# Quantised feed-forward weights rebuilt in the attention stage and kept in HBM, instead of beside their matmuls; a new order of TensorE's work in local attention

## The reference

```python
x = x + tanh(g_xattn[0]) * local_attention(ln(x), ctx)      # 8 heads, window of 16 positions along the 512 axis
x = x + tanh(g_ffn[0])   * routed_lora(ln(x))               # x @ W_base + top-2 of 8 experts of rank 16
x = x + tanh(g_xattn[1]) * rotary_attention(ln(x), ctx)     # 32 query heads, 8 key heads of 128, batches of 64
x = x + tanh(g_ffn[1])   * gated_mlp(ln(x))                 # silu(x @ Wg) * (x @ Wu) @ Wd, 512 -> 1376 -> 512
# the three matrices of the last block are 4-bit numbers, eight packed in an int32 along k:
W[k, n] = scales[g_idx[k], n] * (w4[k, n] - (z4[g_idx[k], n] + 1))
```

## Time and profile before

| | us |
|---|---|
| median of 3 runs | 1184.46 (1182.89 to 1184.77) |
| the profiled execution's own time | 1184.0 |
| its span, first to last instruction | 1182.2 |
| busy: PE, DVE, POOL, ACT | 1065.9, 799.2, 425.9, 363.2 |
| local attention, routed lora | 0 to 268, 268 to 344 |
| rotary attention, gated mlp, down | 344 to 944, 944 to 1118, 1118 to 1182 |

### The profile page before, as it was taken

How to read it: one execution, slowest core, us unless ns; L and a number is a source line. 1 busy time by engine, 2 the same in 40 slices (tenths; PEclk the granted TensorE clock), 3 DMA queues, 4 the chain that set the end, 5 groups by cost and what they waited for, 6 DMA issues and landing times. The chain is left out here.

```text
span 1182.2 us, 13680 instructions
## 1 busy us (share of the span) xinstructions
PE 1065.9 (90%) x4894; PEld 754.7 (64%) x4894; DVE 799.2 (68%) x1230; ACT 363.2 (31%) x938; POOL 425.9 (36%) x262
## 2 busy tenths in 40 slices
PE   5677778778578999999999999999999789999998
PEld 1333333335456777777777777777777457777787
DVE  4888888858876766667677666766665456666423
ACT  3333333213212443334333333432333222111121
POOL 4566666646423433424334233333330012111121
PEclk8888889978788999999999999999999979999999
DMA  8000000000320110101111010110200012111001
GB/s 264 1 1 2 1 1 3 10 0 19 103 57 27 45 45 28 39 26 45 45 29 52 11 63 28 45 45 18 64 1 1 1 43 56 54 54 52 14 1 72
DMA packets 46143, 43.21 MB, mean 37 GB/s; under 512 B 7646, under 2 KB 35046, under 8 KB 46076
## 3 DMA queue, kind: packets, MB, share of 16 engines
q1 hardware_dynamic: 45356, 41.97, 11.7%
q10 hardware_dynamic: 720, 0.36, 0.1%
HBM read 40.22 MB, written 2.10 MB: 36 GB/s over the span
## 5 line engine op out<-in xcount | busy, mean ns | idle before, releaser
L1240 POOL TENSOR_TENSOR shared<-shared 128x512 f32<-128x512 f32 x64 | 82.3, 1286 | 201.6 <-DVE shared L1367 201.4
L1365 DVE TENSOR_TENSOR shared<-ps,cs 128x512 f32<-128x512 f32 x80 | 55.2, 690 | 95.7 <-PE ps L765 95.7
L1302 ACT ACTIVATE c_xn<-c_xn,c_mn 128x64 f32<-128x64 f32 x256 | 86.1, 337 | 106.0 <-DVE c_mn L1381 106.0
L763 PE MATMUL ps<-woh,oh 128*128 128x512 f32 x256 | 103.7, 405 | 5.1 <-DVE ol L1397 5.1
L763 PE MATMUL ps<-xh,wqh 128*128 128x512 f32 x256 | 106.6, 417 | 0.4 <-DVE shared L1367 0.4
L1402 DVE SCALAR_TENSOR_TENSOR x<-ps,gate,x 128x512 f32<-128x512 f32 x64 | 48.0, 751 | 79.4 <-PE ps L765 79.4
L765 PE MATMUL ps<-woh,ol 128*128 128x512 f32 x256 | 101.4, 396 | 0.0
L764 PE MATMUL ps<-wol,oh 128*128 128x512 f32 x256 | 101.2, 395 | 0.0
L765 PE MATMUL ps<-xh,wql 128*128 128x512 f32 x256 | 100.6, 393 | 0.0
L764 PE MATMUL ps<-xl,wqh 128*128 128x512 f32 x256 | 99.9, 390 | 0.0
L549 DVE TENSOR_TENSOR r<-ps,vpad 128x512 f32<-128x512 f32 x128 | 79.4, 683 | 28.8 <-PE ps L638 28.8
(11 more groups left out here) (181 smaller groups left out, 2475.2 us busy)
## 6 DMA issues: line engine op xcount, KB each, us to landing
stage<-in_wq SPq DMA_DIRECT2D x16, 512.0 KB, 3.7
stage<-in_wo SPq DMA_DIRECT2D x16, 512.0 KB, 3.6
qraw<-in_gate_qweight SPq DMA_DIRECT2D x40, 64.0 KB, 2.3
qraw<-in_up_qweight SPq DMA_DIRECT2D x40, 64.0 KB, 2.3
qraw<-in_down_qweight SPq DMA_DIRECT2D x10, 256.0 KB, 3.3
x<-in_x SPq DMA_DIRECT2D x8, 256.0 KB, 6.8
ctxt<-in_ctx SPq DMA_DIRECT2D x8, 256.0 KB, 6.9
stage<-in_wk SPq DMA_DIRECT2D x8, 256.0 KB, 2.8
```

Source lines behind the costliest of these rows:

```text
L763: pe.matmul(dst, lh, rh, start=(first and c == 0), stop=False)
L1240: pool.tensor_tensor(qT[:, h * TPH:(h + 1) * TPH, :, p - 1, :], turn(ra), turn(rb), ALU.add)\
L1302: act.activation(part, part, ACT.Exp, scale=-1.0, bias=mn[:, c % 2, u:u + 1], accum_out=sm[:, c % 2, u:u + 1]).then_inc(exp_ready, 1)
L1365: dve.tensor_tensor(A, bank, cs[:, 0, :].unsqueeze(1).broadcast_to([P, nb, C]), ALU.mult)
```

## The change

The quantised weights are no longer made in the gated mlp. Seven small loads early in local attention bring scales, zeros and indices; in routed lora VectorE builds two tables of scale and zero rows (build_tables, ahead of the choice of experts; nothing is left behind it or between the tiles), and SP stores them in HBM. In the rotary stage a unit is handled in each of the steps 1 to 43 (32 units of 128x344, then 11 of 128x512): SP loads the packed numbers, GpSimd gathers each row's scales and zeros from the table in HBM by an indirect DMA, VectorE unpacks, subtracts and multiplies (three instructions, at three places of its step), and SP stores the result in HBM. The gated mlp loads finished weights in tiles of 128x512 and has no one-hot matmuls, no unpacking, and all eight banks for its products. The splitting of the scales on GpSimd and ScalarE in local attention is gone. There, TensorE spreads three windows before it turns the second half back, and all four reductions stand among the windows.

```diff
-        HEADS_AT = {5: 0, 7: 1}
+        HEADS_AT = {5: (0, 0), 6: (0, 1), 8: (1, 0), 9: (1, 1)}
...
                     turn_back(i, 0)
-                    if s < NT:
-                        reduce_heads(s, 0, 0)
-                        reduce_heads(s, 0, 1)
-                    turn_back(i, 1)
                     if i == 0:
                         pe.wait_ge(spread_ready, 1)
-                    for n in range(WIN):
+                    for n in range(3):
+                        spread_window(i, n)
+                    turn_back(i, 1)
+                    for n in range(3, WIN):
                         spread_window(i, n)
                         if s < NT and n in HEADS_AT:
-                            reduce_heads(s, 1, HEADS_AT[n])
+                            reduce_heads(s, *HEADS_AT[n])
...
-                m, k = (s - 2) // 2, (s - 2) % 2
-                if 0 <= m < 3:
-                    scales_pool(pool, g, m, k)
...
+def build_tables(dve, g, link):
...
+    for rows, cols in ((slice(0, 2 * GK), INTER), (down, D)):
+        for j in range(PACK):
+            last = dve.tensor_scalar(zu[rows, j:cols:PACK], zq[rows, 0:cols // PACK], BITS * j, 15,
+                                     ALU.logical_shift_right, ALU.bitwise_and)
+    link(last)
+    dve.tensor_scalar(table_rows(table)[:, :, 1, :], zu[0:2 * GK, :].rearrange("r (q n) -> r q n", q=QPIECES),
+                      1.0, None, ALU.add)
...
+def gather_scales(pool, g, u):
+
+    if u >= 2:
+        pool.wait_ge(g["w_ready"], u - 1)
+    table, width = (g["table_wide"], 2 * QCOLS) if u < WIDE_UNITS else (g["table_down"], 2 * D)
+    pool.indirect_dma_start(g["sz"][:, u % 2, 0:width], None, table,
+                            bass.IndirectOffsetOnAxis(ap=g["index"][:, u:u + 1], axis=0)).then_inc(g["sz_landed"][u % 2], 16)
...
+def unpack_weights(dve, g, u):
+
+    rows, cols = unit_shape(u)
+    raw = g["qraw"][0:rows, u % 2, 0:cols]
+    dve.wait_ge(g["q_landed"][u % 2], 16 * (u // 2 + 1))
+    dve.tensor_scalar(raw, raw, g["nib"][0:rows, 0:1], 15, ALU.logical_shift_right, ALU.bitwise_and).then_inc(g["qn_ready"], 1)
...
+def subtract_zeros(dve, g, u):
...
+    dve.tensor_tensor(g["dq"][0:rows, u % 2, 0:cols], g["qraw"][0:rows, u % 2, 0:cols], g["sz"][0:rows, u % 2, cols:2 * cols],
+                      ALU.subtract).then_inc(g["q_used"], 1)
...
+def multiply_scales(dve, g, u):
...
+    dve.tensor_tensor(w, w, g["sz"][0:rows, u % 2, 0:cols], ALU.mult).then_inc(g["w_ready"], 1)
...
@@ rotary_attention, SP: a step
+                due = piece_due(c, last)
+                if due:
+                    piece, db, odd = due
+                    load_number(PIECES * (2 * (b + db) + odd) + piece + 2)
+                u = unit_at(n)
+                if u is not None:
+                    if 2 <= u + 2 < Q_UNITS:
+                        load_packed(sp, a, g, u + 2)
+                    store_weights(sp, g, u)
@@ rotary_attention, GpSimd: at the end of a step
+                u = unit_at(step_number(b, c))
+                if u is not None and u + 2 < Q_UNITS:
+                    gather_scales(pool, g, u + 2)
@@ rotary_attention, VectorE: a step
                 if tile_exists(c, last):
                     minimum(b, c)
+                u = unit_at(step_number(b, c))
+                if u is not None:
+                    subtract_zeros(dve, g, u)
...
                 if tile_exists(c, last):
                     probabilities(b, c)
+                if u is not None:
+                    multiply_scales(dve, g, u)
                 for p in units[1:]:
                     rotary(b, sl + 1, p)
+                if u is not None and u + 1 < Q_UNITS:
+                    unpack_weights(dve, g, u + 1)
@@ gate_up
-            zeros_and_scales(0)
-            zeros_and_scales(1)
-            for i in range(NT - 2):
+            for i in range(NT - 1):
                 norm_turn(pe, g, n, xn, XT, i)
-            zeros_and_scales(2)
             pe.wait_ge(n["xl_ready"], TPH)
             products(0, 0, 0)
-            norm_turn(pe, g, n, xn, XT, NT - 2)
             norm_turn(pe, g, n, xn, XT, NT - 1)
             products(0, 0, 1)
-            zeros_and_scales(3)
             pe.wait_ge(n["xl_ready"], NT)
             products(0, 1, 0)
-            zeros_and_scales(4)
             products(0, 1, 1)
             for t in range(1, NTI):
-                zeros_and_scales(3 * t + 2)
                 for hf in range(NHALF):
                     for m in range(2):
-
-                        if t + 1 < NTI and hf == 0:
-                            zeros_and_scales(3 * (t + 1) + m)
                         products(t, hf, m)
```

More of the change, by code:

```diff
@@ L324, in _ @@
             lora_loads(sp, a, g)
-            load_groups(sp, a, g, 0)
-            for m in range(3):
-                load_scales(sp, a, g, m)
-            load_groups(sp, a, g, 1)
+            load_tables(sp, a, g)
         @block.gpsimd
@@ L666, in _ @@
                 if s == 0:
-                    for half in range(2):
-                        for e in range(2):
-                            reduce_heads(0, half, e)
+                    for n in sorted(HEADS_AT):
+                        reduce_heads(0, *HEADS_AT[n])
                     queries(1)
@@ L813, in scales_pool @@
[L813 to L833 removed]
+LORA_LOADS = 7
@@ L1030, in _ @@
             widen(0)
-            for k in range(GROUP_STEPS):
-                groups_of(1, k)
             dve.wait_ge(small_ready, 2 * NHALF)
@@ L1161, in rotary_attention @@
         aT = sb("aT", [P, 2, KEYS])
+        g["qraw"] = sb("qraw", [P, 2, D], I32)
+        g["sz"] = sb("sz", [P, 2, 2 * D])
+        g["dq"] = sb("dq", [P, 2, D])
+        for name in ("qn_ready", "q_used", "w_ready"):
+            g[name] = sem(name)
+        for name in ("q_landed", "sz_landed"):
+            g[name] = [sem(f"{name}{i}") for i in range(2)]
         oh = sb("oh", [P, 2, GRP * P], F32R)
@@ L1258, in _ @@
             low_piece(pool, g, 0, 0, O23)
+            gather_scales(pool, g, 0)
+            gather_scales(pool, g, 1)
+            for c in range(HEAD):
+                step(0, c)
             for b in range(PAIRS - 1):
-                steps(b, False)
-            steps(PAIRS - 1, True)
+                for c in BODY:
+                    step(b, c)
+            for c in BODY:
+                step(PAIRS - 1, c, last=True)
             row_scales(pool, g, st)
@@ new lines, in _ @@
+            for k in range(TILES2):
+                t, m = k // 2, k % 2
+                if k >= 4:
+                    sp.wait_ge(wl_ready, k - 3)
+                sp.dma_start(tile_view(wf, k), wide[m, :, :, t * P:t * P + inner(t)]).then_inc(wf_landed[k % 4], 16)
+                if k == 3:
+                    full = (NTI - 1) * P
+                    sp.dma_start(wd[:, 0:NTI - 1, :], g["w_down"][0:full, :].rearrange("(t p) n -> p t n", p=P))\
+                      .then_inc(wd_landed, 16)
+                    sp.dma_start(wd[0:inner(NTI - 1), NTI - 1, :], g["w_down"][full:INTER, :]).then_inc(wd_landed, 16)
@@ L1759, in _ @@
         def _(pe):
-            def zeros_and_scales(u):
-                t, m = u // 3, u % 3
-                if u >= 2:
-                    pe.wait_ge(unit_ready, u - 1)
-                pieces = [(ROW0[m] + c * P, P, COL0[m] + t * P, c * P, inner(t)) for c in range(DC)]
-                if m == 2:
-                    pieces = [(ROW0[m] + t * P, inner(t), COL0[m], 0, D)]
-                for r0, k, c0, at, width in pieces:
-                    pe.matmul(ps[0:k, Z[u % 2], at:at + width], onehot[96:128, r0:r0 + k], rows[96:128, c0:c0 + width],
-                              start=True, stop=True)
-                    last = pe.matmul(ps[0:k, SC[u % 2], at:at + width], onehot[0:96, r0:r0 + k], rows[0:96, c0:c0 + width],
-                                     start=True, stop=True)
-                last.then_inc(zs_done, 1)
             def products(t, hf, m):
```

384 lines of the change are left out of this document (169 added, 215 removed).

## The result

The changed kernel takes 1172.78 us in the median (1170.97 to 1173.05, 4 runs); the ratio to the kernel before is 0.9903, with a 95% interval of 0.9886 to 0.9920. That is 11 us faster, inside the range given (1136 to 1180), and half of the 21 us that were forecast. The profiled execution took 1172.5 us with a span of 1170.7, so it is compared with the 1184.0 of before: -11.5.

The account below looks back on a forecast made before the run. VectorE was taken to bound local attention, TensorE rotary attention and the gated mlp. The terms -3.3 - 4.1 + 26.6 - 40.6 = -21.4 took 1184.0 to 1162.6, say 1163 us, range 1136 to 1180.

Parts of the forecast that it names:

- Gated mlp, forecast -40.6: Gated mlp: without one-hot matmuls, -33.2 us behind the 13th product and -7.4 at the head, nothing waiting.
- Routed lora, -4.1: Routed lora: choice of experts 3.0 us later for the tables, 7.0 won behind it, -.7 for a last shift and copy.
- Local attention, -3.3: Local attention: -8.6 us from dropping the scale splitting, +5.3 from the new order of TensorE.
- The price of the order: Local attention: reductions among the windows leave VectorE gaps, +.9 us in each of six steps, +5.3 in all.
- The splitting: Local attention: without GpSimd's scale splitting VectorE's L531 isn't held up, -8.2 us; exponentials without ScalarE's copies, -.4.
- Rotary attention, +26.6: Rotary attention: three new VectorE operations mostly fill waits, but stall behind GpSimd's pieces in eleven steps, +26.6 us.
- the piece (to 651.0) catches the new multiply: Rotary attention, worked step with j = 2: GpSimd's piece holds the multiply until 651.4, project_out starts 3.1 us later.
- the two stalls: Rotary attention: 3.1 us in each of five steps with c % 8 = 6, 1.85 in six with c % 8 = 2.
- The other steps have no second piece, and DVE's long waits before L1365 absorb 1.9 us.: Rotary attention: steps outside the two stall patterns lose nothing, as VectorE's waits for projections take in the added work.
- no stall: Rival, rotary attention: the multiply gets in ahead of the queued piece, only 3.5 us lost; total 1139.5, chance .30.
- The slow gather: Rival, rotary attention: the gather takes some 3 us of GpSimd, 38.5 us lost in place of 26.6; 1174.5, chance .17.
- the blocking one: Rival, rotary attention: the gather holds GpSimd 4.8 us with VectorE waiting, +91 us for +26.6; 1227, chance .07.

Follow-up runs that it names:

- d1: Changed kernel with the gated mlp's products in four banks, waiting for the h of tile t - 1 instead of t - 2: 1173.67 us, ratio 0.9913.
- a2: Kernel before, with the new order of TensorE in local attention as its only edit: 1186.38 us against 1183.14, ratio 1.0026.
- u1: Changed kernel with the unpack ahead of the step's second rotation instead of behind it: 1164.08 us, ratio 0.9826.
- g1: Changed kernel without the gathers of units 2 to 42, every unit using the first two units' scales and zeros: 1171.39 us, ratio 0.991.
- u4: Changed kernel with the multiply alone moved right behind subtract, the unpack staying at the step's end: 1171.32 us, ratio 0.9908.
- b1: Changed kernel with all of build_tables moved behind VectorE's product for the first tile in routed lora: 1176.2 us, ratio 0.9931.
- b2: Changed kernel with build_tables split: index part ahead of the choice of experts, table part behind the first tile's product: 1164.3 us, ratio 0.9824.
- a1: Changed kernel with the old order of TensorE in local attention: 1169.43 us, ratio 0.9873.

## Why the prediction was half right

**Gated mlp, forecast -40.6, measured -42.7.** Right in both parts: -34.6 behind the 13th product for -33.2 (the matmuls follow at .227, not .23), -8.1 at the head for -7.4. That nothing should wait held; d1 adds that eight banks were no condition for it.

**Routed lora, -4.1, measured -2.8.** The widened weights reach PE 3.4 us later, counted from the stage's start, for "3.0 later"; behind them 6.2 are won for 7.1. The shifts went at GpSimd's pace, as the earlier trace rows had said.

**Local attention, -3.3, measured -6.0.** Both terms were near, and most of the miss is the one trace of before. The price of the order: +5.3 forecast, 4.4 to 4.9 measured, and the gaps of one step (.27, .74, .58, .73, .34) are those counted (.25, .81, .62, .77, .64) but for the last. The splitting: -8.6 forecast; from the first soft maximum on, the old order without it takes 232.6 and 232.1 us for 241.4, -8.8 and -9.2. That makes -4.4 from there on. The other 1.7 us lie ahead of it: the soft maximum's first operation starts at 25.88 after and 27.56 before. One group of 16 matmuls makes the difference, here in the kernel before and in a2, whose code is the same but for the order:

```profile
21.95 3.64 PE L590 MATMUL ps<-prod,sel 128*32 128x512 f32 x16 [0.79 <-ACT sc L439]
```
```profile
21.23 1.92 PE L590 MATMUL ps<-prod,sel 128*32 128x512 f32 x16 [0.82 <-ACT sc L439]
```

The granted clock from 20 to 28 us was .65 before and .94 after. With before's own loads and memsets a2 starts its first soft maximum at 25.12, so these 1.7 us are the clock of one execution and nothing that the change did.

**Rotary attention, +26.6, measured +40.1.** This is the term that failed. Its mechanism was right as far as it went: "the piece (to 651.0) catches the new multiply" is what the trace shows at ten of its eleven places, and where nothing else disturbs it (u1) the two stalls are 1.4 to 1.9 and 2.5 to 3.1 for my 1.85 and 3.1. PE's idle time ahead of project_out came at 35 us for 32, but by luck: the forecast places held less than reckoned, and places that I had at nothing made it up. The step that failed is the sentence "The other steps have no second piece, and DVE's long waits before L1365 absorb 1.9 us." The waits do absorb the work, but the unpack doesn't stand in front of one. In 20 of the 43 steps it is between the second rotation and low_out, and that rotation is the very thing that starts GpSimd's sum. I had priced it by L1720's .48, a row from a stage where GpSimd is mostly idle, although the same row's maximum was 1.40, which stands beside a GpSimd operation (L1678), and had looked for contention only beside the long pieces, not beside the sums. It cost 15.3 us and took some off the other two patterns, which came to 16.5 in ten steps where 24.8 were reckoned (22.1 in u1). The rest is at the first steps, 6.6 us up to step 4 where I had one stall of 1.85, since my working began only with the steady steps (there L1457 was held 3.91 us, and TensorE came out of its wait of 6.0 at the lower clock), and 1.6 of lower clock at step 24: 15.3 - 8.3 + 4.8 + 1.6 = 13.4, the miss.

On the rivals: "no stall" fell, since the multiply is caught in ten of its eleven steps. The slow gather fell by the group of L856 (.96), and the blocking one by the same group (never over 1.24) and by g1. By the rule of the Trainium skill ("SBUF — State Buffer", section "SBUF: two separate sides") a DMA from GpSimd's queue that takes about 620 ns alone takes about 3100 ns beside a VectorE copy. The time that it holds GpSimd shows nothing of that here: .94 to 1.24 in 43 cases. Whether its transfers came later for it no run here separates; nobody waited for them in the changed kernel. The same section says that VectorE and GpSimd lock each other out of the shared port for whole instructions when VectorE has two SBUF inputs or runs in a two-port mode. The first half agrees with the multiply's 2.73, the second would cover the unpack's 1.52 and up to 2.52 (u4), if it ran in such a mode, which no trace here names.

The total came out nearer than the largest term, because the smaller terms erred the other way by 3.5 us, 1.7 of it the clock of the one trace of before. That is luck. The parts are what was tested.

## What to carry over

When work is put into an engine's idle time, the average of that idle time says little: look at what the instruction directly ahead releases on another engine, and put the new work where the engine itself waits, not between a release and the next thing on the critical path. The same three operations cost 40 us at their first places and 8 at others (with their loads moved ahead of the blocked one). Moving a consumer forward in its list needs the same look at the list that feeds it: behind a blocked load on SP, a move that should have given 30 us cost 52.

## What the hardware showed that was not expected

- An operation of VectorE with a single tensor operand in SBUF (int32, 128x344) is held up by GpSimd like one with two: 1.52 beside a sum, up to 2.52 beside a piece, .39 alone. Very small ones can be too: in b1 and b2 operations of 8 to 64 columns took 1.0 to 1.4 us beside GpSimd's burst, others there .2. It can go the other way: beside an unpack of .40 the sum took 1.50 for 1.28 (u4).
- An indirect DMA of 128 rows of 2752 bytes held GpSimd .96 us; one of 4096 bytes, .96 as well.
- A stall may be paid in advance: u1 removed 15.3 us in twenty steps, and the steps behind them grew by 5.6.
- The granted clock differs between executions in places whose code is the same: 16 matmuls took 3.64 us in one trace and 1.92 in another, and the first 65 us of rotary attention, with the same code, ran at .90 in the changed kernel and at .84 in a1, whose stage took 3.7 us more. A difference of 2 to 4 us between two traces of a stage is not yet an effect of the edit.
